# Residual rows stored ahead, and expert tiles that add themselves to them through an accumulating store

## What is computed

```python
h = layernorm(x) * (1 + ca) + sa
x = x + ga * attention(h)                        # "x2" in the kernel
h = layernorm(x) * (1 + cb) + sb                 # "h2"
e = argmax(h @ router_w)                         # one of 14 experts
w = softmax(h @ router_w)[e]
x = x + gb * w * (gelu(h @ w1[e] + b1[e]) @ w2[e] + b2[e])
```

## Time and profile before

| | |
|---|---|
| time, median of 3 runs | 610.19 us (608.88 to 610.45) |
| profiled execution | span 609.1 us from its first to its last instruction; its time is told by that span alone |
| busy: ACT, DVE, PE, POOL | 90%, 91%, 77%, 80% |
| attention stage | to about 492 us |
| tile stage, visits 4 to 76 | about 510 to 602 us |
| moved by DMA | 94.42 MB |

### The profile page before, as it was taken

One profiled execution on the slowest core, in us unless ns is written; L12 is line 12 of the kernel. 1 busy time (PEld: TensorE's weight loads), 2 busy tenths in 40 slices (PEclk: granted clock), 3 DMA queues, 4 the chain that ended last, 5 costly groups with the idle time before them and its releaser, 6 DMA issues.

```text
span 609.1 us, 12013 instructions
## 1 busy us (share of the span) xinstructions
PE 471.5 (77%) x2535; PEld 266.9 (44%) x2537; DVE 555.4 (91%) x1419; ACT 545.2 (90%) x2323; POOL 484.3 (80%) x642
## 2 busy tenths in 40 slices
PE   5456887877887777788788788778776688989993
PEld 2113433333343333333334343334333366889992
DVE  5898999999999999999999999999999978788884
ACT  2599999999999999999999999999999963767882
POOL 4566777998999989899998989989898765677763
PEclk9555556566556756655655655675555565999997
DMA  6365544544455555555555555665555215888750
GB/s 194 104 189 157 138 140 125 139 138 140 141 149 148 148 152 140 163 142 167 146 156 149 148 154 148 173 172 145 160 149 152 93 65 143 269 281 255 223 180 27
DMA packets 77072, 94.42 MB, mean 155 GB/s; under 512 B 12806, under 2 KB 60710, under 8 KB 76998
## 3 DMA queue, kind: packets, MB, share of 16 engines
q1 hardware_dynamic: 68842, 75.69, 45.0%
q0 software_dynamic: 6144, 16.82, 7.4%
q10 hardware_dynamic: 2015, 1.15, 0.7%
HBM read 58.41 MB, written 35.20 MB: 154 GB/s over the span
## 4 chain that ended last, share of the span: by engine, by line
ACT 48%; POOL 17%; DVE 12%; PE 11%; issue 8%; DMA 2%; ACTq 1%; POOLq 0%; DVEq 0%; SPq 0%
ACT scores L927 47%; DVE neg_max L1395 4%; PE scores L1223 4%; PE scores L1232 4%; POOL table L838 3%; POOL xhat L787 2%; POOL rstd L770 2%; POOL rest L577 2%; POOL parts L580 2%; POOL h_scaled L810 1%; DVE y_biased_s L1966 1%; DMA table<-rows,place_i 1%; PE scores L1213 1%; POOL xhat L779 1%; POOL att L799 1%
## 5 line engine op out<-in xcount | busy, mean ns | idle before, releaser
L927 ACT ACTIVATE scores<-scores,neg_max 128x256 f32<-128x256 f32 x1024 | 468.5, 827 | 10.5 <-DVE neg_max L1395 10.4
L927 ACT ACTIVATION_READ_ACCUMULATOR scores<-scores,neg_max 128x1 f32 x1024 | 436.2, 588 | 0.0
L1395 DVE TENSOR_REDUCE neg_max<-scores 128x4 f32<-128x1024 f32 x256 | 309.2, 1211 | 7.5 <-PE scores L1073 7.0
L1073 PE MATMUL scores<-k_stack,q_stack 64*128 64x256 bf16 x1024 | 148.5, 389 | 79.3 <-ACT scores L927 67.7
L1073 PEld LDWEIGHTS scores<-k_stack,q_stack 64*128 64x128 bf16 x1024 | 34.0, 106 | 164.3 <-ACT scores L927 120.6
L838 POOL DMA_INDIRECT table<-rows,place_i x64 | 66.0, 1031 | 20.4 <-issue 17.0
L787 POOL TENSOR_SCALAR xhat<-rows,mv,rstd 128x128 f32<-128x128 f32 x60 | 47.6, 796 | 7.1 <-POOL rstd L770 7.1
L893 POOL DMA_INDIRECT out_dram<-x_s x40 | 39.4, 986 | 17.4 <-DVE x_s L1977 9.2
L1232 PE MATMUL scores<-w_s,hid 128*128 x308 | 49.8, 286 | 2.2 <-DVE y_biased_s L1966 1.1
L1101 PE MATMUL side_a<-w_gated,opt_t 128*128 128x128 f32 x128 | 49.7, 491 | 0.0
L779 POOL TENSOR_SCALAR xhat<-x_s,mv,rstd 128x128 f32<-128x128 f32 x62 | 49.1, 801 | 0.4 <-POOL rstd L770 0.4
(11 more groups left out here) (231 smaller groups left out, 876.0 us busy)
## 6 DMA issues: line engine op xcount, KB each, us to landing
q_stack<-parts_dram SPq DMA_DIRECT2D x192, 64.0 KB, 2.9
x_s<-table SPq DMA_DIRECT2D x62, 192.5 KB
parts_dram<-parts SPq DMA_DIRECT2D x31, 384.0 KB, 3.0
k_stack<-parts_dram SPq DMA_DIRECT2D x186, 64.0 KB, 2.2
mod_b<-mod_rows SPq DMA_DIRECT2D x32, 256.0 KB, 4.4
x_s<-in_x_dram SPq DMA_DIRECT2D x13, 256.0 KB, 4.8
table<-pad_tile SPq DMA_DIRECT2D x15, 192.5 KB
more_rooms<-table SPq DMA_DIRECT2D x15, 192.5 KB
```

Source lines behind the costliest of these rows:

```text
L927: last = act.activation(buf[:, k * L:k * L + L], buf[:, k * L:k * L + L], ACT.Exp, bias=neg_max[:, p, n:n + 1], accum_out=exp_sum[:, p, n: ...
L1073: last = pe.matmul(scores[:, c, at:at + L], q_stack[p][r, g + j, t * P:t * P + P], k_stack[p][r, g + j, :], start=True, stop=True)
L1395: dve.tensor_reduce(to, scores[:, (PAIRS * b.n + i) % RING, :].rearrange("p (e j m) -> p e j m", e=2, j=2), AX_X, ALU.max, negate=True).th ...
```

## The change

x2 leaves the table row. It lives in a ring of two buffers of its own and is stored by SP straight to its place in the output, once per batch; a table row is 257 words. An expert tile's store then adds (gate * (y + b2)) to the output rows that are there, so that VectorE has no sum to form: `gate_y` writes its product into the room. Rooms are 28 instead of 21, all over the storage of x. GpSimd waits for the x2 stores ahead of its first stores; SP stores the x2 of the last two batches in `fill_ends`. The waits for a free row buffer move from `residual` to where h2 is written.

```diff
-H2, X2, GW, ID = 0, D, 2 * D, 3 * D
-ROW = 3 * D + 1
+H2, GW, ID = 0, D, 2 * D
+ROW = 2 * D + 1
-MORE = 5
-ROOMS = SLOTS + MORE
+ROOMS = 28
+RING_X2 = 2
...
+            def store_x2(b):
+                r = b.slot(RING_X2)
+                sp.wait_ge(x2_ready, b.done())
+                sp.dma_start(out_tiles[:, LT * b.n:LT * b.n + LT, :], x2[r][:, :, :]).then_inc(x2_stored[r], 16)
...
+                if b.ago(2).there():
+                    store_x2(b.ago(2))
                 if b.ago(-2).there():
                     store_parts(b.ago(-2))
...
             def fill_ends():
+                store_x2(Batch(B - 2))
+                store_x2(Batch(B - 1))
...
             def modulate2(b):
                 pool.wait_ge(xhat2_ready, b.done())
+                need(pool, scattered[b.slot(RING_ROWS)], 16 * LT * b.earlier(RING_ROWS))
...
                 scatter(last.ago(2), range(1, LT))
+                for r in range(RING_X2):
+                    pool.wait_ge(x2_stored[r], 16 * len(range(r, B - 2, RING_X2)))
                 store(0)
...
                 pool.indirect_dma_start(out_rows, bass.IndirectOffsetOnAxis(ap=room[:, ID:ROW].bitcast(I32), axis=0),
-                                        room[:, GW:GW + D], None).then_inc(out_stored[n % SLOTS], 16)
+                                        room[:, GW:GW + D], None, compute_op=ALU.add).then_inc(out_stored[n % SLOTS], 16)
...
             over_batches(iteration, drain)
+            for r in range(RING_X2):
+                pool.wait_ge(x2_stored[r], 16 * len(range(r, B, RING_X2)))
             for n, k in STORES[FIRST:]:
...
-                r = b.slot(RING_ROWS)
-                need(dve, scattered[r], 16 * LT * b.earlier(RING_ROWS))
-                dve.tensor_tensor(rows[r][:, :, X2:X2 + D], x2_p.rearrange("p (t d) -> p t d", t=LT),
+                r = b.slot(RING_X2)
+                need(dve, x2_stored[r], 16 * b.earlier(RING_X2))
+                need(dve, xhat2_ready, b.n - 1)
+                dve.tensor_tensor(x2[r][:, :, :], x2_p.rearrange("p (t d) -> p t d", t=LT),
                                   x_s[:, ds(LT * b.n, LT), :], ALU.add).then_inc(x2_ready, 1)
...
             def gate_y(n):
+                values = rows_in[n % ROOMS][:, GW:GW + D]
                 dve.wait_ge(y_biased, n + 1)
-                dve.tensor_tensor(y_gated_s[:, n % 2, :], y_biased_s[:, n % 2, :], rows_in[n % ROOMS][:, GW:GW + D],
-                                  ALU.mult).then_inc(y_gated, 1)
-
-            def out_y(n):
-                room = rows_in[n % ROOMS]
-                dve.wait_ge(y_gated, n + 1)
-                dve.tensor_tensor(room[:, GW:GW + D], y_gated_s[:, n % 2, :], room[:, X2:X2 + D], ALU.add).then_inc(out_ready, 1)
+                dve.tensor_tensor(values, y_biased_s[:, n % 2, :], values, ALU.mult).then_inc(out_ready, 1)
...
                     if in_range(n):
                         bias_y(n)
                     if n > PRIMED + 1:
-                        out_y(n - 1)
-                    if in_range(n):
-                        gate_y(n)
+                        gate_y(n - 1)
```

More of the change, by code:

```diff
@@ L78 @@
 W1X = F + FH
+assert ROOMS * ROW + (BUFS_W1 - BUFS) * W1X <= T * D
 X_LATE = 12
@@ L310, in build_adaln_attention_moe @@
         out_rows = out.rearrange("b l d -> (b l) d")
+        out_tiles = out.rearrange("b (t p) d -> p (b t) d", p=P)
         ident_s = sb("ident_s", [P, P])
@@ L346, in build_adaln_attention_moe @@
         x_s = sb("x_s", [P, T, D])
-        more_rooms = sb("more_rooms", [P, MORE, ROW])
         q_stack = [sb(f"q_stack{p}", [P, HALF, L], BF16) for p in range(2)]
@@ L370, in build_adaln_attention_moe @@
         rows = [sb(f"rows{r}", [P, LT, ROW]) for r in range(RING_ROWS)]
+        x2 = [sb(f"x2_{r}", [P, LT, D]) for r in range(RING_X2)]
         logit_s = sb("logit_s", [P, 2 * LT, E])
@@ L423, in build_adaln_attention_moe @@
         packed_now = sb("packed_now", [1, 2 * SLOTS], I32)
-        rows_in = [x_room[:, s * ROW:s * ROW + ROW] for s in range(SLOTS)]
-        rows_in += [more_rooms[:, s, :] for s in range(MORE)]
+        rows_in = [x_room[:, s * ROW:s * ROW + ROW] for s in range(ROOMS)]
         x_t = sb("x_t", [P, BUFS, P])
         w1_ring = sb("w1_ring", [P, BUFS, W1X])
-        after_rows = SLOTS * ROW
+        after_rows = ROOMS * ROW
         w1_e = [w1_ring[:, k, :] for k in range(BUFS)]
@@ L432, in build_adaln_attention_moe @@
         y_biased_s = sb("y_biased_s", [P, 2, D])
-        y_gated_s = sb("y_gated_s", [P, 2, D])
         scores = ps("scores", [P, RING, 1024])
@@ L515, in build_adaln_attention_moe @@
         x2_ready = sem("x2_ready")
+        x2_stored = [sem(f"x2_stored{r}") for r in range(RING_X2)]
         xhat2_ready = sem("xhat2_ready")
@@ L548, in build_adaln_attention_moe @@
         y_biased = sem("y_biased")
-        y_gated = sem("y_gated")
         out_ready = sem("out_ready")
@@ L786, in normalise_x2 @@
                 for t in range(LT):
-                    last = pool.tensor_scalar(xhat2[:, t, :], rows[b.slot(RING_ROWS)][:, t, X2:X2 + D], mv[:, 1, t, 0:1],
+                    last = pool.tensor_scalar(xhat2[:, t, :], x2[b.slot(RING_X2)][:, t, :], mv[:, 1, t, 0:1],
                                               rstd[:, 1, LT + t:LT + t + 1], ALU.subtract, ALU.mult)
@@ L899, in store_packed @@
                 pool.indirect_dma_start(out_rows, bass.IndirectOffsetOnAxis(ap=packed[:, k, D:OUT], axis=0),
-                                        packed[:, k, 0:D].bitcast(F32), None).then_inc(packed_stored, 16)
+                                        packed[:, k, 0:D].bitcast(F32), None, compute_op=ALU.add).then_inc(packed_stored, 16)
             over_batches(iteration, drain)
+            for r in range(RING_X2):
+                pool.wait_ge(x2_stored[r], 16 * len(range(r, B, RING_X2)))
             for n, k in STORES[FIRST:]:
@@ L1330, in x2_row @@
             def x2_row(b, t):
-                return rows[b.slot(RING_ROWS)][:, t, X2:X2 + D]
+                return x2[b.slot(RING_X2)][:, t, :]
             def stats_x(b):
@@ L1370, in shift_h2 @@
                 dve.wait_ge(rstd_ready, count)
+                need(dve, scattered[b.slot(RING_ROWS)], 16 * LT * b.earlier(RING_ROWS))
                 steps.after(step["scaled"])
@@ L1965, in bias_y @@
                 dve.wait_ge(y_done, n + 1)
+                need(dve, out_ready, n - 1)
                 dve.tensor_tensor(y_biased_s[:, k, :], expert_out[k],
@@ L1990, in whole_y @@
                 gate_y(n)
-                out_y(n)
             def tile(j, s, turn):
```

## The result

The kernel with the change takes 636.85 us (median of 6 runs, 635.41 to 638.48), the kernel before in the same session 609.54 (607.33 to 610.76): a ratio of 1.0456, 95% interval 1.0431 to 1.0481. It is slower by 27.3 us, where 605.8 us with a range up to 620 had been forecast. The profiled execution took 638.42 us with a span of 636.6, against 609.1 before.

A forecast was written before the change was run, and what follows sets the result against it. Bounds: ScalarE in attention, then TensorE's visits with gaps, GpSimd within 2 us of bounding the tile stage. 2.1 + 2.6 + 0.65 - 1.0 = 4.35 us off the 609.1 span gives 604.7; from the median 605.8, range 603.5 to 620.

The forecast's parts named there:

- GpSimd's pace: Tile stage, GpSimd's stores: an accumulating store takes as long to issue as a plain one, 0.96 us; 0 us added.
- The slower rival: Accumulating stores issue longer on GpSimd, perhaps 1.44 us in place of 0.96, giving 630.6 us; chance 0.31.
- the last scatter: Last table-row scatter, before visit 12's load: lands 1.8 us sooner because the bytes queued with it shrink by a third.
- GpSimd's slack: Tile stage: GpSimd has 2.1 us left before its stores bound the forecast time.
- 2.6 us for the beats: VectorE in the tile stage: without its sums, gaps between TensorE's visits and at the last product shrink by 2.6 us.
- 0.65 at the end: After the last product: two sums go and VectorE is less late, gaining 0.65 us.
- the drain: `out_y(0)` on VectorE, ahead of the copy TensorE waits for at 503.94 us: its removal gains 0.3 us.
- the second rival: Issue 0.09 to 0.14 us longer (608.7 to 611.5 us), or late last scatter with VectorE's gaps staying (610.1); chance 0.12.
- What was costed at nothing: x2 stores on SP, GpSimd's new waits, loads of 128.5 KB and 28 rooms: no effect on the time.
- The landing of an accumulating store: Output store at the kernel's end: reading before writing makes it land 1.0 us later, counted once.
- The rival that VectorE's relief leaves the gaps: Tile-stage gaps follow register loads and ScalarE, so they stay despite less VectorE work: 608.4 us; chance 0.07.
- The one of a little longer issue: Same as the second rival: an issue 0.09 to 0.14 us longer gives 608.7 to 611.5 us; chance 0.12.

The follow-up runs named there:

- e7: Changed kernel with accumulating stores of only 64 of the 128 words of each of 128 rows: 635.8 us (one run).
- e8: Kernel before with only the 13 packed stores of shared tiles accumulating: 614.6 us against 609.58, ratio 1.0079.
- e10: Changed kernel with plain stores and its 14 closing pad stores one per visit from visit 16 on: 603.46 us against 608.71, ratio 0.9916.
- e4: Kernel before with no pad stores ahead of the load of visit 12, one per visit from visit 16 on: 608.82 us, ratio 1.0008.
- e9: Kernel before without the sum on VectorE, the gate written in place; long rows, 21 rooms and plain stores stay: 605.69 us against 608.71, ratio 0.9945.
- e1: Changed kernel with plain stores in place of accumulating ones, all else kept: 605.6 us against 609.17, ratio 0.9942.
- e11: Changed kernel with plain stores and a GpSimd memset ahead of every store: 628.68 us, ratio 1.0331.
- e12: Kernel before with its 14 closing pad stores one per visit from visit 22 to 35: 610.63 us, ratio 1.0022.

## Why the prediction was wrong, step by step

**The step that failed** is "GpSimd's pace", and in it the sentence "I take 0, by the nearest row: what the issue costs has followed neither bytes nor packets." The size is 0.59 us (1.547 against 0.96). The row of the scatter (1540-byte rows in 0.963 us) was read rightly, and e7 confirms it: the issue does not follow bytes. But both rows are plain stores. They say how the cost varies with the size of the same operation and nothing of a change of the operation, and of that cost 0.44 us are fixed, whatever the number of rows. Sitting beside a slack of 2.1 us, multiplied by 56, a term with no row of its own should not have had half of the chance at zero.

**The slower rival was right in mechanism, and in its formula.** With the measured size it gives 56 x 0.587 - 2.1 = 30.8 us on the forecast of 605.8, so 636.6 us; 636.85 were measured. That they agree so closely is luck in part. By the formula the last store starts at 594.3 + 32.9 = 627.2 us, with 8.3 us from there to the end of the span; measured were 630.04 and 6.6. Store 7 started at 525.23 us, not 522.6, since the gain at the last scatter did not come, and the end was shorter than forecast. The two errors nearly cancel. Its price of 0.48 was too low, and the range, cut at 0.3, left out the case altogether. The reading of "Perfetto Trace Analysis", section "DMA Instruction — SWDGE (GPSIMD)", in the Trainium skill, that the slice ends with the last generated descriptor, so that more of them would lengthen it, is in keeping with the trace: the slice grew, and so did the packets, from 16 to 128 for a store, though not in proportion.

**GpSimd's slack: right in size.** 2.1 us forecast, 2.6 absorbed in e8, with an interval of 1.1 to 4.6. It is not quite the same slack: in e8 only the 13 late stores are longer.

**The last scatter: wrong.** 1.8 us were taken, because bytes shrink by a third; it landed no sooner with short rows (6.1 to 7.4 against 5.3 to 6.1). That the six pads delay it was right (at most 2.9 us without them), that their time goes by bytes was not. The view that carries it, share beside GB/s, could have been asked of the kernel before. The rule of "DMA: Bandwidth & Descriptors", section "Anatomy of one DMA — SWDGE (gpsimd) path", in the Trainium skill, came nearer with its 0.15 us, though a landing of 6 to 7 us is not what it describes. And an earlier load had less to give than the gap of 1.4 us: the register load of the expert numbers in front of the same transpose leaves some 0.35 us of it (e10), and in e4, where the load is issued 3.5 us sooner against TensorE's work, all 1.44. The prediction speaks of gaps by register loads, and did not look for one here.

**VectorE: right.** 2.6 us for the beats and 0.65 at the end, 3.25 together; e9 shows 3.0. In the changed kernel the beats from 531.79 to 538.99 us are of 1.00 with one exception, and the gain is then lost in the queue on GpSimd. The 0.3 us of the drain lies within these 3.0 and was not separated. (Two slips that change nothing: 522.73 us is the transpose of visit 12, and the first product of visit 8 comes half a microsecond later; and the 610.1 of the second rival adds up to 610.2.)

**What was costed at nothing: right, as far as it can be measured.** x2 stores, new waits, table loads of 128.5 KB and 28 rooms: e1 and e9 agree within their intervals, and attention iterations are as long as they were.

**The landing of an accumulating store: too large.** The medians do not part it from other load on the queues: from 515 us on, plain stores land after 2.4 us before, 3.1 in e1 and 3.0 in e11, accumulating ones after 3.4. The shortest landings are 2.2, 2.2 and 2.3 us against 3.2; 0.6 of that is the longer issue, so some 0.4 is the transfer's, where 1.0 was taken. The end of the kernel agrees. From the last store's end of issue to the end of the span there are 5.0 us after (630.04 + 1.55 to 636.6) and 6.4 before (601.75 + 0.96 to 609.1). Of these, 3.0 and 4.8 are SyncE's last wait for TensorE's queue, which leaves 2.0 and 1.6. Why that wait is shorter is not shown.

**The rival that VectorE's relief leaves the gaps: wrong**, by e9. The one of a little longer issue had the mechanism, and not the size.

## What to carry to other kernels

Where an engine has two microseconds of slack over fifty repeated operations, an operation on it that no row shows decides the outcome: measure its issue once, by itself in one kernel, before anything else of the change is costed. A row of another kind of the same instruction shows how the cost follows size, and not what a new mode adds. And when an accumulation in the DMA is to take a 0.28 us sum from one engine, look at what the issuing engine pays: here 0.59 us each on the one with the least slack in the tile stage. A gap that the trace puts down to one cause can have a second one right behind it: look also at what the profile does not count as busy, register loads here.

## What the runs showed of the hardware

- An indirect store of 128 rows of 512 bytes from GpSimd took 0.96 us to issue plain and 1.547 us with addition in the DMA. With 64 rows it was 0.90 and 1.41; with rows of 256 bytes, accumulating, still 1.547 (one run each).
- The plain store went as 16 packets, the accumulating one as one packet a row. Between two indirect DMAs GpSimd paused 0.30 us in either case.
- A scatter of 128 rows landed within 2.9 us with no pad stores in front (e4, e10, e12). With six in front it took 5.3 to 6.1 us with rows of 1540 bytes and 6.1 to 7.4 us with rows of 1028: a third fewer bytes in as many packets of the pads brought nothing.
- A load of up to 16 expert numbers into TensorE's registers took 1.1 to 1.5 us in the tile stage, and 2.3 and 3.0 us once each (e4, e12). In these two and in e10 the gap on TensorE ended 0.1 to 0.2 us behind it. What makes it longer was not found.
